# Patch embedding over full tiles of a stream of all images, with its rows kept in device memory

## What is computed

```python
hidden = jnp.einsum('npd,hd->nph', patches, W_lin) + b_lin       # 196 rows of 192 for an image
h = jnp.concatenate([cls, hidden, txt], axis=1)                  # 325 tokens
h = h + attention(layernorm(h))      # 12 heads of 16, rms norm of q and k, rotary, causal
h = h + ffn(layernorm(h))            # shared expert + 2 of 3 routed ones, 192 -> 384 -> 192
```

## Time and profile before

| | us |
|---|---|
| median of 3 runs | 1747.44 |
| lowest, highest | 1746.33, 1747.51 |
| the profiled execution | 1748.54 |
| its span, first to last instruction | 1746.7 |
| busy: PE, weight load, DVE, ACT, POOL | 1657.0, 1549.5, 1220.3, 981.8, 407.1 |
| mean granted clock of TensorE | 0.979 |

### The profile page before, as it was taken

How to read it: one execution, slowest core, us unless ns; L and a number is a source line. 1 busy time by engine, 2 the same in 40 slices (tenths; PEclk the granted TensorE clock), 3 DMA queues, 4 the chain that set the end, 5 groups by cost and what they waited for, 6 DMA issues and landing times.

```text
span 1746.7 us, 47388 instructions
## 1 busy us (share of the span) xinstructions
PE 1657.0 (95%) x17280; PEld 1549.5 (89%) x17280; DVE 1220.3 (70%) x3480; ACT 981.8 (56%) x2113; POOL 407.1 (23%) x647
## 2 busy tenths in 40 slices
PE   3589999999999999999999999999999999999998
PEld 3479999999999999999999999999999999999887
DVE  4467777677777677777667777767777767777754
ACT  1565555666555666555566555565555566655541
POOL 0222122222112222112222112222212222211220
PEclk8689999999999999999999999999999999999999
DMA  4000000000000000000000000000000000000000
GB/s 168 7 24 30 30 23 14 20 29 29 29 23 18 16 29 29 29 29 23 12 23 29 29 29 23 13 21 29 29 29 23 14 20 29 29 29 15 9 7 12
DMA packets 26705, 45.65 MB, mean 26 GB/s; under 512 B 2381, under 2 KB 17586, under 8 KB 26546
## 3 DMA queue, kind: packets, MB, share of 16 engines
q1 hardware_dynamic: 26674, 45.22, 7.8%
HBM read 27.79 MB, written 7.99 MB: 20 GB/s over the span
## 4 chain that ended last, share of the span: by engine, by line
PE 90%; ACT 3%; DVE 3%; issue 2%; SPq 1%; DMA 0%; POOL 0%; POOLq 0%; DVEq 0%; ACTq 0%
PE ps L317 79%; PE ps L486 6%; PE ps L320 5%; ACT k_split L592 1%; ACT route_e L673 1%; DVE wf L1000 0%; ACT q_split L592 0%; DMA probs<-in_w_route 0%; ACT rows L596 0%; DVE wf L998 0%; DVE xt L788 0%; DVE stats L777 0%; SPq L270 0%; DVE rotated L843 0%; POOL rstd L710 0%
## 5 line engine op out<-in xcount | busy, mean ns | idle before, releaser
L317 PE MATMUL ps<-xt,wf 64*128 64x326 f32 x6912 | 590.8, 315 | 9.0 <-issue 8.6
L317 PEld LDWEIGHTS ps<-xt,wf 64*128 64x128 f32 x6912 | 521.0, 186 | 14.1 <-issue 12.1
L317 PE MATMUL ps<-w_down_s,ht 128*128 128x192 f32 (+1 forms) x2304 | 416.4, 331 | 2.2 <-DVE ht L745 1.6
L317 PEld LDWEIGHTS ps<-w_down_s,ht 128*128 128x128 f32 (+1 forms) x2304 | 354.8, 175 | 20.7 <-DVE ht L745 1.9
L739 DVE SCALAR_TENSOR_TENSOR gated<-tanh_g,ps 128x326 f32<-128x326 f32 x384 | 189.2, 493 | 224.1 <-ACT tanh_g L603 224.1
L596 ACT ACTIVATE rows<-h,rstd 128x192 f32<-128x192 f32 (+2 forms) x288 | 155.0, 561 | 229.8 <-POOL rstd L714 229.8
L603 ACT ACTIVATE tanh_g<-ps 128x326 f32<-128x326 f32 x384 | 170.3, 443 | 169.6 <-PE ps L317 168.2
L703 POOL TENSOR_TENSOR probs<-probs,causal 128x512 f32<-128x512 f32 x192 | 228.9, 1192 | 129.5 <-ACT probs L614 129.5
L614 ACT ACTIVATE probs<-ps 128x792 f32<-128x792 f32 (+1 forms) x384 | 254.4, 662 | 6.5 <-PE ps L317 6.5
L697 POOL TENSOR_TENSOR probs<-probs,causal 69x140 f32<-69x140 f32 x192 | 89.7, 467 | 572.5 <-ACT probs L614 572.5
L745 DVE TENSOR_TENSOR ht<-gated,ps 128x326 f32<-128x326 f32 x384 | 190.1, 495 | 13.1
(11 more groups left out here) (96 smaller groups left out, 2196.9 us busy)
## 6 DMA issues: line engine op xcount, KB each, us to landing
x_s<-in_xp SPq DMA_DIRECT2D x32, 591.0 KB, 3.8
residual<-h SPq DMA_DIRECT2D x32, 288.0 KB, 2.3
out<-o SPq DMA_DIRECT2D x32, 192.0 KB
h<-in_txt SPq DMA_DIRECT2D x32, 51.8 KB
out<-o SPq DMA_DIRECT2D x32, 51.8 KB
ht<-in_w_ffn SPq DMA_DIRECT2D x2, 768.0 KB, 7.2
h<-in_txt SPq DMA_DIRECT2D x32, 44.2 KB
w_down_s<-in_w_down SPq DMA_DIRECT2D x1, 1152.0 KB, 10.5
```

Source lines behind the costliest of these rows:

```text
L317: return nc.tensor.matmul(dst, lhs, rhs, start=first, stop=last)
```

## The change

The patches of all images become one stream of 32 x 196 = 6272 rows, cut into 25 steps of 256 (`STEPS`); the last is filled up with zeros. A step is embedded as two full tiles of 128 rows, twelve written matmuls as before. DVE adds the bias into a new tile `embed_rows` in one operation, SP stores it to `kept_rows` in device memory, and the 196 rows of an image are loaded from there into `h0`, one partition down, by two DMAs of 127 and 69 partitions. Image 0 takes its rows from `embed_rows` directly, by three DMAs. The class token is loaded once into row 0 of `h0`.

A turn now has the flags D (the rows of a step are still awaited), E (a step is embedded), T (an image is loaded), L, A, F. E is false from turn 23 on. In such turns PE does `down(3,0)` and `down(3,1)` where the embedding stood, into the embedding's PSUM bank, ahead of `norm2_turn`; their sum moves to where `embed_sum` stood on DVE. Turns -1 to 1, 22, 23 and 30 to 32 are written out, 2 to 21 and 24 to 29 are two loops. In turns -1 to 1 the load of an image waits for the store of the step embedded in that turn; later it stands behind the residual copy and waits for the step before. The experts' weights are still split between turns -1 and 0.

```diff
+STEPS = -(-BATCH * PATCHES // (2 * P))
-        bias_rows = sb("bias_rows", [P, 2, DIM])
+        bias_rows = sb("bias_rows", [P, DIM])
-        x_s = sb("x_s", [P, KT, SEEN])
+        x_s = sb("x_s", [P, 2, KT, P])
+        embed_rows = sb("embed_rows", [P, 2, DIM])
-        def accumulator(e, t):
+        def accumulator(e, t, E=True):
+            if e == FFNS - 1 and t < 2 and not E:
+                return ps[:, EMBED_BANK, t * DIM:(t + 1) * DIM]
...
+        def turns(engine, turn):
+            for i in (-1, 0, 1):
+                turn(i, True, True, True, True, i >= 0, i >= 1)
+            with engine.Fori(2, STEPS - 3) as i:
+                turn(i, True, True, True, True, True, True)
+            turn(STEPS - 3, True, True, True, True, True, True)
+            turn(STEPS - 2, True, False, True, True, True, True)
+            with engine.Fori(STEPS - 1, BATCH - 2) as i:
+                turn(i, False, False, True, True, True, True)
+            for i in range(BATCH - 2, BATCH + 1):
+                turn(i, False, False, False, i + 1 < BATCH, i < BATCH, True)
...
-            sp.dma_start(bias_rows[1:P, 0, :], bias.partition_broadcast(P - 1)).then_inc(s_const, 16)
-            sp.dma_start(bias_rows[0:SEEN1, 1, :], bias.partition_broadcast(SEEN1)).then_inc(s_const, 16)
-            sp.dma_start(bias_rows[0:1, 0, :], cls).then_inc(s_const, 16)
+            sp.dma_start(bias_rows[:], bias.partition_broadcast(P)).then_inc(s_const, 16)
             sp.wait_ge(s_clear, 1)
+            sp.dma_start(h0[0:1, 0, :], cls).then_inc(s_const, 16)
...
+            def store_rows(step):
+                sp.wait_ge(rows_added.sem, rows_added.at(step, 1))
+                sp.dma_start(step_rows[step], embed_rows[:]).then_inc(rows_stored.sem, 16)
+            def load_hidden(i, step, D):
+                b0, b1 = i + 2, i + 1
+                sp.wait_ge(n1_applied.sem, n1_applied.at(b1, 1))
+                sp.wait_ge(res_copied.sem, res_copied.at(b1, 16))
+                if D:
+                    sp.wait_ge(rows_stored.sem, rows_stored.at(step, 16))
+                sp.dma_start(h0[1:P, 0, :], batch_rows[b0, 0:P - 1, :]).then_inc(hidden_loaded.sem, 16)
+                sp.dma_start(h0[0:SEEN1, 1, :], batch_rows[b0, P - 1:PATCHES, :]).then_inc(hidden_loaded.sem, 16)
+                sp.dma_start(h0[SEEN1:P, 1, :], txt[b0, 0:TXT1, :]).then_inc(txt_loaded.sem, 16)
+                sp.dma_start(h0[0:REAL2, 2, :], txt[b0, TXT1:TXT, :]).then_inc(txt_loaded.sem, 16)
...
                     sp.dma_start(residual[:], h0[:]).then_inc(res_copied.sem, 16)
+                late = isinstance(i, int) and i < 2
+                if T and not late:
+                    load_hidden(i, i + 1, D)
...
                     sp.dma_start(x_s[:], xp[b0 + 1]).then_inc(x_loaded.sem, 16)
+                if E:
+                    store_rows(b0)
+                if T and late:
+                    load_hidden(i, i + 2, D)
...
             sp.dma_start(x_s[:], xp[1]).then_inc(x_loaded.sem, 16)
+            sp.wait_ge(rows_added.sem, rows_added.at(0, 1))
+            sp.dma_start(h0[1:P, 0, :], embed_rows[0:P - 1, 0, :]).then_inc(hidden_loaded.sem, 16)
+            sp.dma_start(h0[0:1, 1, :], embed_rows[P - 1:P, 0, :]).then_inc(s_first, 16)
+            sp.dma_start(h0[1:SEEN1, 1, :], embed_rows[0:SEEN1 - 1, 1, :]).then_inc(hidden_loaded.sem, 16)
+            store_rows(0)
...
-                for t, n in enumerate((P, SEEN1)):
+                for t in range(2):
                     for j in range(KT):
-                        last = mm(ps[0:n, EMBED_BANK, t * DIM:(t + 1) * DIM], x_s[:, j, t * P:t * P + n],
+                        last = mm(ps[:, EMBED_BANK, t * DIM:(t + 1) * DIM], x_s[:, t, j, :],
                                   w_tok_s[:, j, :], j == 0, j == KT - 1)
...
                 if E:
                     embed(b0)
-                if F:
-                    pe.wait_ge(summed.sem, summed.at(b3, 4))
+                    if F:
+                        pe.wait_ge(summed.sem, summed.at(b3, 4))
+                else:
+                    down(3, 0, b3, E)
+                    down(3, 1, b3, E)
                 if A:
                     norm2_turn(b2)
                 if F:
                     pe.wait_ge(summed.sem, summed.at(b3, 6))
+                if F and E:
                     down(3, 0, b3)
                     down(3, 1, b3)
...
-                for t, n in enumerate((P, SEEN1)):
-                    v.tensor_tensor(h0[0:n, t, :], ps[0:n, EMBED_BANK, t * DIM:(t + 1) * DIM],
-                                    bias_rows[0:n, t, :], ALU.add).then_inc(h0_ready.sem, 1)
+                    dve.wait_ge(rows_stored.sem, rows_stored.at(b - 1, 16))
+                v.tensor_tensor(embed_rows[:], ps[:, EMBED_BANK, 0:QK].rearrange("p (t d) -> p t d", t=2),
+                                shaped(bias_rows[:], [[0, 2], [1, DIM]]), ALU.add).then_inc(rows_added.sem, 1)
...
                 if E:
                     embed_sum(b0)
+                elif not (isinstance(i, int) and i == BATCH):
+                    sum_up(6, b3, E)
```

More of the change, by code:

```diff
@@ L162, in build @@
         s_power = ctx.enter_context(nc.semaphore("power_kept"))
+        s_first = ctx.enter_context(nc.semaphore("first_row_moved"))
         s_halve = ctx.enter_context(nc.semaphore("down_halved"))
@@ L250, in build @@
         block = ctx.enter_context(nc.Block())
[L252 to L263, removed]
+        step_rows = kept_rows.rearrange("(s t p) d -> s p t d", t=2, p=P)
+        batch_rows = kept_rows[0:BATCH * PATCHES].rearrange("(b n) d -> b n d", n=PATCHES)
+        def turns(engine, turn):
[9 more added lines that the diff above has]
+                turn(i, False, False, False, i + 1 < BATCH, i < BATCH, True)
         @block.sync
@@ L309, in _ @@
             sp.dma_start(x_s[:], xp[1]).then_inc(x_loaded.sem, 16)
-            first_turns(turn)
-            turns(sp, turn, BATCH - 3)
+            sp.wait_ge(rows_added.sem, rows_added.at(0, 1))
[3 more added lines that the diff above has]
+            store_rows(0)
+            turns(sp, turn)
             sp.wait_ge(stored.sem, stored.at(BATCH - 1, 32))
@@ L505, in route_turn, with down @@
                 last.then_inc(route_turned.sem, 1)
-            def down(e, t, b):
+            def down(e, t, b, E=True):
                 if t == 0 and e == 0:
@@ L515, in down, with turn @@
                     last.then_inc(down_done.sem, 1)
-            def turn(i, E, L, A, F):
+            def turn(i, D, E, T, L, A, F):
                 b0, b1, b2, b3 = i + 2, i + 1, i, i - 1
+                if F and not later(b3):
+                    pe.wait_ge(s_ffn_split, 2 * SPLIT_PARTS)
+                    pe.wait_ge(s_halve, 2)
                 for k in range(UNITS):
                     if F:
-                        unit(k, b3, L, A)
+                        unit(k, b3, D, A)
                     if A:
@@ L578, in _ @@
             embed(0)
-            pe.wait_ge(s_const, 16 * 8)
+            pe.wait_ge(s_const, 16 * 7)
             pe.wait_ge(s_rows_split, 6)
             pe.wait_ge(s_halve, 1)
[L582 to L586, removed]
             turns(pe, turn)
@@ L909, in route_pick, with split_ffn, turn @@
                 last.then_inc(pick_chain.sem, 1)
-            def turn(i, E, L, A, F):
+            def split_ffn():
+                for j in range(SPLIT_PARTS):
+                    u = slice(SPLIT_AT[j], SPLIT_AT[j + 1])
+                    dve.wait_ge(s_ffn[j], 16)
+                    v.tensor_copy(wf[:, u, :, 0, :], raw_f[j]).then_inc(s_ffn_split, 1)
+                    dve.wait_ge(s_ffn_split, 2 * j + 1)
+                    v.tensor_tensor(wf[:, u, :, 1, :], raw_f[j], f32(wf[:, u, :, 0, :]), ALU.subtract).then_inc(s_ffn_split, 1)
+                dve.wait_ge(s_down, 16)
+                v.tensor_scalar(w_down_s[:], w_down_s[:], 0.5, None, ALU.mult).then_inc(s_halve, 1)
+            def turn(i, D, E, T, L, A, F):
                 b0, b1, b2, b3 = i + 2, i + 1, i, i - 1
+                if isinstance(i, int) and i == 0:
+                    split_ffn()
                 if F and later(b3):
-                    sum_up(6, b3 - 1)
+                    if D:
+                        sum_up(6, b3 - 1)
                     sum_up(7, b3 - 1)
@@ L921, in turn @@
                         dve.wait_ge(txt_loaded.sem, txt_loaded.at(b1, 32))
-                        dve.wait_ge(h0_ready.sem, h0_ready.at(b1, 2))
+                        dve.wait_ge(hidden_loaded.sem, hidden_loaded.at(b1, 32))
+                        if isinstance(i, int) and b1 == 0:
+                            dve.wait_ge(s_first, 16)
                         moments(h0, stats, stats_chain, b1, rstd, mean_var, n1_moments)
@@ L993, in _ @@
             v.tensor_tensor(wr[H:P], raw_r[H:P], f32(wr[H:P]), ALU.subtract).then_inc(s_rows_split, 1)
[L994 to L1004, removed]
             turns(dve, turn)
-            sum_up(6, BATCH - 1)
+            sum_up(6, BATCH - 1, False)
```

47 lines of the change are left out of this document (23 added, 24 removed).

## The result

The changed kernel takes 1762.78 us (median of 4 runs, 1760.99 to 1763.55) against 1746.96 us before: ratio 1.0088, 95% interval 1.0076 to 1.0101. It is slower, as forecast, by 15.8 us where 7.8 were forecast. The profiled execution is the fastest of the four (1760.99, span 1759.1, 12.4 us above the span of the profiled execution before), so what follows explains 12.4 us, and the other runs lie up to 2.6 higher.

A forecast was written before the change was run, and what follows sets the result against it. PE held 90% of the chain, but DVE and ACT were taken to bound the stretch around the embedding. Terms 2.9 + 8.2 + 1.5 - 3.4 - 0.6 - 0.8 = +7.8 gave 1755.2 us on the median's scale, range 1746 to 1766.

The forecast's parts named there:

- turn 31: Turn 31, from down(2,*) to the next unit: 11.0 us instead of 14.38 with both downs ahead of norm2_turn, -3.4 us.
- PE's 27.3 us: Turns 23 to 29: PE loses 27.3 us of embedding work, nearly all off the path, becoming idle time.
- The price of the low clock in turns 23 to 29: Idle time costs clock as in turn 30, 0.60 us per turn; less the 0.18 gain, +2.9 us over seven turns.
- the order: Turns 23 to 29: with two downs ahead of norm2_turn, the router starts at about 9.38 instead of 9.56, gain 0.18 per turn.
- the first rival: Turns 23 to 29: the clock stays low through the q/k transposes, costing 14 us in place of 2.9; total 1766, chance 0.15.
- The start: Before turn 1: image 0's rows land at 29.05 and the first statistics start 8.2 us late, +8.2 us.
- the queue: At the start: image 0's rows come behind xp[1], itself queued behind the weights and landing at 27.75 before the change.
- one engine for 127 partitions: At the start: a 127-partition DMA goes by one engine, about 145 rows, 111 KB at 23 GB/s, 4.8 us.
- the bias rows: At the start: two bias DMAs go, one of which held SP's queue for 3.98 us; weights may come 4 us earlier.
- Rows through device memory: Turn 1: rows for the next image land at 166.6, DVE is 2.5 us late, PE feels +1.5 us.
- The end: Turn 30: 0; turn 31: -3.4 us; last turn without its 0.60 us wait before the last downs: -0.6 us.
- The loop boundaries: Three more turn boundaries leave the loop, at 0.28 us each, -0.8 us; -0.6 of this over turns 3 to 22.

The follow-up runs named there:

- the shortened embedding: Kernel before, with 10 of the 12 written matmuls of the embedding left out in turns 23 to 29: 1746.53 us, ratio 0.9996.
- the idle embedding: Changed kernel, with 24 unused embedding matmuls in turns 23 to 30 and down(3,0), down(3,1) behind norm2_turn again: 1755.69 us, ratio 1.0041.
- even parts: Changed kernel, with image rows loaded as 112 + 15 and 64 + 5 (4) partitions instead of 127 and 69 (68): 1755.64 us, ratio 1.0044.
- first experiment: Changed kernel, with image 0's rows issued ahead of the experts' weights and xp[1]: 1752.84 us, ratio 1.0027.
- the downs spread over the gaps: Changed kernel, with down(3,1) and down(3,2) between norm2_turn and the router in turns without embedding: 1763.27 us, ratio 1.0089.
- the late sums: Changed kernel, turns 23 to 30: DVE's two sums of expert 2 behind low_part(1), all three downs of expert 3 ahead of norm2_turn: 1769.01 us, ratio 1.0114.
- The version with four fillers: Changed kernel with early image 0 rows, rows in even parts, late sums and four unused matmuls before the router in turns 23 to 30: 1744.85 us, ratio 0.9973.
- nine fillers: As the version with four fillers, but nine unused matmuls in PE's gaps and down(3,2) behind the router: 1735.92 us, ratio 0.9935.

## Why the prediction was right, point by point

The direction and the two main mechanisms were right, and the time fell into the range. The size was half of what came, and one of the terms that matched (turn 31) did so largely for another reason than the one given.

- **PE's 27.3 us are off the path: right.** The two gaps stood at 0.90 and 2.48 us; the shortened embedding and the idle embedding show it in either kernel.
- **The price of the low clock in turns 23 to 29: too small.** The step "I take turn 30's price, since the gap is of that size", 7 x 0.42 = +2.9, measured +5.9 against the old turns (with one loop boundary less), and +6.1 against the idle embedding, where the clock stayed up. The mechanism was right, the term mis-sized: in three of seven turns the clock stayed low for 6.8 us, twice as long as in turn 30. The one turn 23 of the changed order in which the clock held took 51.25 (even parts), 0.4 less than a written-out turn before, so by an estimate from it the low clock cost about 1.3 us per turn where 0.60 was taken, and the order gained 0.4 where 0.18 was taken. That turn 30's gap lay before `down` matmuls and the new one before the router and transposes may be why; that was the first rival's argument and no run isolates it. Its 14 us were too much, the truth lies between.
- **The start: right**, +8.3 against +8.2, with its parts: the queue (first experiment), one engine for 127 partitions (second), the bias rows (3.7 us where 4.0 were taken). That SP's queue would stand for 10.29 us was not seen; it delayed the issue of the last of the three DMAs to 24.43, at the time when the forecast has the rows begin to move.
- **Rows through device memory: right in place, low in size.** The statistics of turn 2 waited 3.12 us (forecast 2.5) and PE 2.17 of them (1.5). The store was quicker than taken (2.1 for 2.6 us), the loads slower (9.8 for 8.5). The term also left the clock out: of the six traces with these undivided rows three have turn 2 at 54.4 to 54.5 us, and three, in which the clock fell in it for 3.4 us, at 56.1 to 56.2.
- **Turn 1, +1.0, was not forecast.** The rows arrived in time; before, the low clock at its start ended at about 109, after, it lasted until about 119, 4 us into the turn. In the version with the idle embedding, which has the same start, turn 1 took 52.78. It goes with where the low clock happens to end, in all twelve traces: turn 1 takes 52.5 to 52.8 us in the seven in which the low clock reaches 1.9 to 2.5 us into it, and 53.5 to 53.9 in the five in which it reaches 4.1 to 5.0. One of these five is the kernel before with its bias rows in even parts (53.54), so the 1.0 us does not come from the rows.
- **The end: right in number**, -4.4 against -4.0, and partly by luck. The 14.38 us of turn 31 before contain 6.8 us at the low clock, while the forecast's 11.0 were summed up from rows at full clock, without a word on why the clock should hold. In the kernel before with the shortened embedding, whose turn 31 is unchanged, the clock happened to hold there, as this line against the earlier trace rows shows:

```profile
1703.72 1.04 PE L322 MATMUL ps<-ident,rows 128*128 128x128 f32 x9 [2.70 <-ACT rows L598]
```

That turn 31 took 43.27 us, against 46.25 before and 42.90 in the changed kernel: the new order of the downs is worth 0.4 of the 3.4, and the clock the rest. With 3.4 us of low clock the old order took 44.93 and the new one 44.5.
- **The loop boundaries:** -0.9 against -0.6 over turns 3 to 22.
- **The remaining 3.4 us** between the profiled difference (12.4) and the medians' (15.8): 1.6 of them lie in the kernel before, whose profiled execution (1748.54) was that much slower than the median of its runs (1746.96). The other 1.8 lie in the changed kernel, whose profiled execution was its fastest. Its two slowest runs, at 1763.5, had a mean granted clock of 0.967 and 0.968 against 0.969, so more low clock goes with them; a turn 2 in which the clock falls would be 1.7, but no trace of those runs shows it.

## What to carry to other kernels

Before removing work from an engine that is 95% busy, find a stretch of the trace where that work is already absent; here one turn in the kernel before gave the answer. Idle time on TensorE is not free even off the critical path: against the same turns with the gap filled, 3.4 us of it per turn cost 0.9 us, and filler matmuls gave that back. Before a term is taken from a row, read the granted clock in that row: a low clock that happens to hold or to fall moved single turns by 1 to 3 us here. Count the partitions of each DMA: 112 + 15 in place of 127, and 64 + 4 in place of 68, landed 3.8 us sooner, and small loads on a critical path belong ahead of the large ones in the queue (8.4 us here).

## What was not expected of the hardware

- The granted clock fell with gaps of 1.87 us and less (the downs spread over the gaps) and of 1.46 and less (the late sums), with transposes close by, and stayed at 0.5 for up to 10.2 us while PE was 93% busy (the window of the late sums above). The Trainium skill ("TensorE: Matmul & The Clock Gate", the section on oscillation) describes such falls behind long DMA waits. In this case's traces they also came behind waits of 0.4 to 2.5 us on DVE and ACT.
- The version with four fillers ran from 1736 to 1752 us on one chip, and the mean granted clock of its runs from 0.980 down to 0.969 with it; with nine fillers the runs lie within 5 us, at 0.979 to 0.983.
- A DMA of one partition held SP's queue for 10.29 us behind one of 127 partitions and the weights. With the weights behind them it took 1.06, and in even parts the longest of these issues took 0.92.
